# A Mamba block between two expert networks on one core: inverse roots on ScalarE, B and C projected in four column groups, a seventh C product on GpSimd, scans ahead of products on VectorE

## The reference

```python
x = x + 0.5 * ffn(layernorm(x))      # "f1"
x = x + mamba(layernorm(x))          # "p"
x = x + 0.5 * ffn(layernorm(x))      # "f2"

# ffn: argmax over 8 gates picks one expert of 128 -> gelu -> 128
# mamba(x):
xn = rmsnorm(x) * norm_w             # 128 channels
xs, z = split(xn @ in_proj.T)        # 256 + 256
xs = silu(causal_conv4(xs) + b)
dt_x, B, C = split(xs @ x_proj.T)    # 128, 16, 16
dt = softplus(dt_x @ dt_proj.T + b)
h  = exp(dt * A) * h + (dt * xs) * B # for each of 256 x 16 states, along the tokens
y  = sum_n(h * C) + D * xs
return (y * silu(z)) @ out_proj.T + x
```

## Time and profile before

| what | value |
|---|---|
| median of 3 runs | 1233.87 us (1229.54, 1233.87, 1234.02) |
| profiled execution, its time | 1229.34 us |
| its span, first to last instruction | 1227.5 us |
| mean granted TensorE clock | 0.936 of full speed |
| busy in the span | PE 1085.6, DVE 1033.3, POOL 1026.2, ACT 916.8 us |

### The profile page before, as it was taken

How to read it: one execution, slowest core, us unless ns; L and a number is a source line. 1 busy time by engine, 2 the same in 40 slices (tenths; PEclk the granted TensorE clock), 3 DMA queues, 4 the chain that set the end, 5 groups by cost and what they waited for, 6 DMA issues and landing times.

```text
span 1227.5 us, 16326 instructions
## 1 busy us (share of the span) xinstructions
PE 1085.6 (88%) x5188; PEld 553.7 (45%) x5188; DVE 1033.3 (84%) x1681; ACT 916.8 (75%) x1349; POOL 1026.2 (84%) x756
## 2 busy tenths in 40 slices
PE   6897859798989999998989999998989996977778
PEld 3352425253535444554545445454545443423245
DVE  2318998899999989999999999998999999999910
ACT  2457576788989888888879888888889796774631
POOL 1248998989899998999998999989899999999600
PEclk9897969799999999999999999999999997958789
DMA  4052324324142423333151433242250424342000
GB/s 102 1 177 85 137 104 140 112 82 161 29 156 104 146 103 140 104 125 136 51 177 61 146 106 146 95 156 104 73 184 24 166 86 146 99 153 95 1 9 18
DMA packets 60406, 130.03 MB, mean 106 GB/s; under 512 B 7744, under 2 KB 26864, under 8 KB 52128
## 3 DMA queue, kind: packets, MB, share of 16 engines
q1 hardware_dynamic: 60320, 128.98, 30.5%
HBM read 106.94 MB, written 22.02 MB: 105 GB/s over the span
## 4 chain that ended last, share of the span: by engine, by line
DVE 43%; PE 27%; ACT 12%; issue 11%; POOL 6%; DVEq 0%; DMA 0%; POOLq 0%; ACTq 0%
DVE dA L986 19%; DVE hb L984 8%; PE PY L619 7%; DVE hb L990 6%; PE PH L586 5%; PE G L567 4%; ACT hs L801 3%; DVE stat L965 3%; POOL hb L1158 2%; PE Y L631 2%; PE dA L599 2%; PE Y L664 2%; ACT xn L758 2%; ACT dA L825 2%; DVE xs L1003 2%
## 5 line engine op out<-in xcount | busy, mean ns | idle before, releaser
L1158 POOL TENSOR_TENSOR hb<-dtx_rep,bs 128x1024 f32<-128x1024 f32 x256 | 598.2, 2359 | 4.9 <-PE Y L631 4.4
L825 ACT ACTIVATE dA<-dt_rep,A 128x512 f32<-128x512 f32 x512 | 344.5, 688 | 105.4 <-DVE hb L990 83.6
L986 DVE TENSOR_TENSOR_SCAN dA<-dA,hb 128x512 f32<-128x512 f32 x320 | 390.2, 1219 | 8.1 <-DVE oh L1028 3.2
L619 PEld LDWEIGHTS PY<-W,hs 128*128 128x128 f32 x2048 | 259.2, 194 | 82.4 <-issue 73.0
L619 PE MATMUL PY<-W,hs 128*128 128x128 f32 x2048 | 293.7, 288 | 0.0
L1166 POOL TENSOR_TENSOR hb<-hb,cs 128x1024 f32<-128x1024 f32 x96 | 225.9, 2361 | 35.0 <-DVE hb L984 35.0
L990 DVE TENSOR_TENSOR hb<-dA,cs 128x512 f32<-128x512 f32 x320 | 221.4, 692 | 22.6 <-DVE dA L986 0.5
L984 DVE TENSOR_TENSOR_SCAN hb<-dA,hb 128x512 f32<-128x512 f32 x192 | 223.5, 1205 | 15.9 <-ACT dA L825 15.8
L586 PE MATMUL PH<-xnT,W 128*128 128x512 f32 x396 | 230.4, 665 | 0.0
L779 ACT COPY hs<-PH 128x512 f32<-128x512 f32 x198 | 114.7, 579 | 106.0 <-PE PH L586 86.9
L631 PE MATMUL Y<-hb,Sel 128*32 128x512 f32 x1024 | 151.8, 664 | 34.6 <-POOL hb L1166 33.7
(11 more groups left out here) (103 smaller groups left out, 1225.5 us busy)
## 6 DMA issues: line engine op xcount, KB each, us to landing
dtx_rep<-dtx_rows SPq DMA_DIRECT2D x32, 1024.0 KB, 6.3
dt_rep<-dt_rows SPq DMA_DIRECT2D x32, 1024.0 KB, 8.0
bs<-bc_rows SPq DMA_DIRECT2D x64, 256.0 KB, 3.7
cs<-bc_rows SPq DMA_DIRECT2D x64, 256.0 KB, 3.6
dtx_rows<-dtx SPq DMA_DIRECT2D x32, 256.0 KB, 2.4
dt_rows<-dt SPq DMA_DIRECT2D x32, 256.0 KB, 2.4
X<-in_x SPq DMA_DIRECT2D x16, 256.0 KB, 3.1
out<-X SPq DMA_DIRECT2D x16, 256.0 KB, 2.4
```

Of the source, the lines that this page charges most:

```text
L619: last = nc.tensor.matmul(PY[:, P * j:P * (j + 1)], hs[:, w, e, P * j:P * (j + 1)], W2[:, e, :], start=False, stop=e == E - 1 and j == J - 1)
L825: nc.scalar.activation(dA[u % NA][:, :], dt_rep[:, h, g, :], ACT.Exp, scale=A[:, h, g, q:q + 1]).then_inc(decay, 1)
L986: nc.vector.tensor_tensor_scan(a, a, x_in_hb, 0.0, ALU.mult, ALU.add).then_inc(scan, 1)
L1158: nc.gpsimd.tensor_tensor(hb[:, s % HR], dtx_rep[:, h, 2 * m:2 * m + 2, :], bs[:, q, None, :].broadcast_to([P, 2, CH]), ALU.mult).then_inc ...
```

## The change

Four things are changed.

1. `inverse_root`: in steady iterations ScalarE makes the root for f1 and f2 as `exp(-0.5*ln(var+eps))` on 4 columns, two instructions that wait on each other (`log_and_root`, at ACT slots 12.5 and 4.5), and GpSimd only negates the mean and multiplies. For p, GpSimd makes both roots in one `pow` of 8 columns, from var+eps and from a variance that is put together first. The f2 root's place on GpSimd is slot 6.5, before 5.5.
2. The products with the bias rows of W2 (L617) come all four ahead of the first expert's four products, before one by one between them. The projection onto B and C is made as eight matmuls of 32 x 128 in four column groups, before two of 32 x 512, and so the copy to SBUF is 128 x 128 instead of 32 x 512; the DMA that stores it writes the same bytes from 128 partitions.
3. Slot 4 joins POOL_C: its C product goes from VectorE to GpSimd, where it stands one slot later than the others do, in slot 6, ahead of slot 5's.
4. VectorE makes both scans of a slot and then both products, before scan, product, scan, product.

```diff
@@ STEADY
-    act={"silu": 3.0, "bc": 4.0, ..., "norm_f2": 7.5, "res_p": 13.5, ...
+    act={"silu": 3.0, "bc": 4.0, ..., "norm_f2": 7.5, "root_f2": 4.5, "root_f1": 12.5, "res_p": 13.5, ...
-    pool={"root_f2": 5.5, "dt": 7.0, "dtx": 7.5, "root_p": 11.0, "norm_p": 11.0, "root_f1": 12.5},
+    pool={"root_f2": 6.5, "dt": 7.0, "dtx": 7.5, "root_p": 11.0, "norm_p": 11.0, "root_f1": 12.5},
...
-POOL_C = (1, 2, 5, 9, 12, 14)
+POOL_C = (1, 2, 4, 5, 9, 12, 14)
+LATE_C = (4,)
...
+                for j in range(J if e == 0 else 0):
+                    nc.tensor.matmul(PY[:, P * j:P * (j + 1)], ohT[:, w, (it.i0 + off) % 2, P * j:P * (j + 1)],
+                                     b_part[:, 1, :], start=j == 0, stop=False)
                 for j in range(J):
-                    if e == 0:
-                        nc.tensor.matmul(PY[:, P * j:P * (j + 1)], ohT[:, w, (it.i0 + off) % 2, P * j:P * (j + 1)],
-                                         b_part[:, 1, :], start=j == 0, stop=False)
...
-                    product(it, "bc", 2 * N, [(Wbc[:, h, :], xsc[:, h, :]) for h in range(HF)])
+                    for h in range(HF):
+                        for g in range(GG):
+                            last = nc.tensor.matmul(G[b][2 * N * g:2 * N * (g + 1), 0:P], Wbc[:, h, :],
+                                                    xsc[:, h, P * g:P * (g + 1)], start=h == 0, stop=h == HF - 1)
...
+            def log_and_root(it, w, off):
+
+                k = 2 * act_roots(w, it.i0 + off)
+                it.wait(act, moments[w], off, 1, 1)
+                it.wait(act, normed[w], off, 1, 0)
+                nc.scalar.activation(vt[:, w, :], mv[:, w, :, 1], ACT.Ln, bias=eps[:, 0:1]).then_inc(log_root[w], 1)
+                act.wait_ge(log_root[w], k + 1)
+                nc.scalar.activation(rstd[:, w, :], vt[:, w, :], ACT.Exp, scale=-0.5).then_inc(log_root[w], 1)
...
-            def state_unit(it, u):
+            def state_scan(it, u):
...
+            def state_products(it, s):
+
                 if s in POOL_C:
                     return
+                q = place(s)[1]
+                it.wait(dve, c_in[q], 0, 16, 16)
+                for u in (2 * s, 2 * s + 1):
+                    it.wait(dve, scan, 0, UN, u + 1)
+                    nc.vector.tensor_tensor(hb[:, s % HR, u % 2, :], dA[u % NA][:, :], cs[:, q, :], ALU.mult) \
+                        .then_inc(prod, 1)
...
                     if it.has(0):
-                        state_unit(it, 2 * s)
+                        state_scan(it, 2 * s)
                     stages(it, s + 0.25)
                     if it.has(0):
-                        state_unit(it, 2 * s + 1)
+                        state_scan(it, 2 * s + 1)
+                        state_products(it, s)
...
+            def inverse_roots_p(it, off):
...
+                nc.gpsimd.tensor_tensor(roots[:, :, :], var[:, :, :], half[:, :, :], ALU.pow).then_inc(pool_ln[2], 1)
```

More of the change, by code:

```diff
@@ L208, in direct_no, with root_on_act, act_roots, roots_before @@
     return E * DIRECT.index((w, chunk)) + e
+def root_on_act(w, chunk):
+    return plan_of(chunk - ROOT_OFF[w]) is STEADY
+def act_roots(w, chunk):
+    return sum(root_on_act(w, c) for c in range(chunk))
+def roots_before(w, chunk):
+    return sum(1 if root_on_act(w, c) else 3 for c in range(chunk))
 def on_pool(s):
@@ L560, in transposes, with product @@
                 last.then_inc(g_full[b], 1)
-            def product(it, name, rows, terms):
+            def product(it, name, terms):
                 b = BANK[name]
@@ L566, in product @@
                 for k, (lhsT, rhs) in enumerate(terms):
-                    last = nc.tensor.matmul(G[b][0:rows, :], lhsT, rhs, start=k == 0, stop=k == len(terms) - 1)
+                    last = nc.tensor.matmul(G[b][:, :], lhsT, rhs, start=k == 0, stop=k == len(terms) - 1)
                 last.then_inc(g_full[b], 1)
@@ L742, in _, with copy_out @@
         def _(act):
[L743 removed]
+            def copy_out(it, name, dst, n=CH):
                 b = BANK[name]
                 it.wait_full(act, g_full, name)
[L747 removed]
+                nc.scalar.copy(dst, G[b][:, 0:n]).then_inc(g_free[b], 1)
             def rows(it, off, j):
@@ L837, in stages @@
                         copy_out(it, f"ln_f{w + 1}", xnT[:, w, :])
+                if t == at.get("root_f2") and it.has(-1):
+                    log_and_root(it, 1, -1)
+                if t == at.get("root_f1") and it.has(4):
+                    log_and_root(it, 0, 4)
                 if t == at.get("norm_f2") and it.has(-1):
@@ L1120, in inverse_root @@
                     .then_inc(pool_ln[w], 1)
-                nc.gpsimd.tensor_tensor(vt[:, w, :], mv[:, w, :, 1], eps[:, 0], ALU.add).then_inc(pool_ln[w], 1)
-                it.wait(pool, pool_ln[w], off, m, 2)
-                nc.gpsimd.tensor_tensor(rstd[:, w, :], vt[:, w, :], half[:, :], ALU.pow).then_inc(pool_ln[w], 1)
-                it.wait(pool, pool_ln[w], off, m, 3)
-                if w < 2:
-                    nc.gpsimd.tensor_tensor(shift[:, w, :], neg[:, w, :], rstd[:, w, :], ALU.mult).then_inc(rooted[w], 1)
-                    return
@@ L1199, in body @@
                         state_bx(it, 0, u)
-                    off, t = (0, s - 1) if s else (-1, SLOTS - 1)
-                    if it.has(off) and t in POOL_C:
-                        product_c(it, off, t)
+                    for back in (2, 1):
+                        off, t = (0, s - back) if s >= back else (-1, SLOTS + s - back)
+                        if it.has(off) and t in POOL_C and (t in LATE_C) == (back == 2):
+                            product_c(it, off, t)
                     stages(it, s + 0.5)
```

78 lines of the change are left out of this document (43 added, 35 removed).

## The result

The changed kernel takes 1241.14 us (median of 5 runs, 1240.23 to 1241.30) against 1233.87 for the kernel before in 5 runs (1229.1 to 1235.82). The ratio is 1.0069, with a 95% interval from 1.0043 to 1.0094: it is slower by 0.7%. The profiled execution took 1240.82 us, with a span of 1239.0 and a mean granted TensorE clock of 0.915.

What follows compares the result with a forecast made beforehand. VectorE, GpSimd and TensorE, each 94% busy, bound the kernel through their waits for each other. Ten iterations at -0.57 (-5.7) and -5 at fill and end: 1233.9 - 10.7 = 1223, put at 1222; 8 in 10: 1206 to 1240.

Steps and rivals of the forecast that it cites:

- third case: TensorE's longer wait after the taps: half clock in each iteration delays the next gelus by 2.4; 1243 us, chance 0.16.
- Sum: Whole kernel: -5.7 us over ten steady iterations and -5 in fill and end, so 1233.9 - 10.7 = 1223.
- this rival: TensorE's wait after the taps: the clock falls in every iteration, seven more falls at 1.4; 1233 us, chance 0.2.
- The rest of the sum: One steady iteration: slot 10 starts 1.2 earlier, then +0.1, +0.89 and -0.36, giving -0.57 us.
- Slots 10 to 14: dA banks come free 0.89 later: unit 24 is 0.1 later and the convolution starts 0.89 later.
- Slot 15, "0.36 less": Slot 15 ends 0.36 us earlier and starts the next gelus, by unit 31's product, last in either order.
- Slot 3: Products 6 and 7 stand behind the output projection's add: 0.5 us more from the add to slot 4.
- TensorE's gain, 1.2: Before slot 10: bias products save 0.8, B and C 0.7, less 0.3 for slot 4's late C product.
- VectorE would begin slot 10 earlier, but its add needs TensorE: VectorE could begin slot 10 1.95 us earlier, but TensorE is back to back from slot 1 to slot 11.
- GpSimd: Seventh product +2.3, roots -3.6, net -1.3 us an iteration; pow of 8 takes 2.0, waits up some 3.
- Fill and drain, -5: Outside the steady iterations: p root twice at -1.2, bias products about 1, VectorE freer at the end; together -5 us.
- ring free: ScalarE's slack hides the later dA banks, so VectorE's 4.8 counts: 2.5 us an iteration; 1204 us, chance 0.14.

Runs made afterwards that it cites:

- changed, filled: The changed kernel with three zero-weight float32 matmuls added in TensorE's wait ahead of slot 15's first expert product, iterations 2 to 12: 1222.12 us.
- the mixed one: The changed kernel with scan, product, scan, product in slots 0, 3, 10, 13 and both scans first in slots 6, 7, 8, 11, 15: 1211.48 us.
- the control: The mixed one with three zero-weight matmuls in iterations 2 to 12, placed in slot 7, where TensorE doesn't stand: 1239.08 us.

## Why the prediction was wrong

The prediction was 1222 us, faster; the outcome is that of its third case, "The same, and slower", 1243, which it gave 0.16. It lies 1.1 us above the range for 8 in 10, 1206 to 1240.

**The step that failed: the clock in "Sum".** The sum carried the falls of before over unchanged. The prediction had itself worked out that the stand would grow, by 0.8 because TensorE comes earlier and by 0.89 because ScalarE comes later, but then treated what follows as a rival. The stand grew by 1.0, and each iteration has a fall. Of its two terms the first came and the second hardly did: TensorE's edits made the stand 0.87 longer in the kernel before (1.91 to 2.78) and the new order 0.16 (1.91 to 2.07). In the changed kernel the stand ends 1.06 later behind slot 10's add, as ScalarE is that much later, but TensorE doesn't come earlier: behind that add it waits 0.36 for slot 9's C product and 0.83 instead of 0.37 for a copy, and so it reaches the stand 20.66 us behind the add, where it was 20.64, although the bias products save it 0.9 in between. The price of the falls comes from filling: 69.86 - 68.05 = 1.8 us an iteration for the changed kernel, 68.38 - 67.8 = 0.6 for before. Of the 1.48 us by which an iteration became longer, 1.2 is the clock. "HAM oscillation" on the page "TensorE: Matmul & The Clock Gate" of the Trainium skill, which the prediction set beside this rival, was the better guide: the traces of the changed kernel agree with it in direction, with ten falls in ten iterations and none once the stand is filled. They don't agree in all: the waits in the page's example are longer than the 2.95 us here, and in the kernel before a stand of 1.91 had a fall in four iterations of ten, not each time.

**The rest of the sum: -0.57 forecast, about +0.2 measured.** This is read from marks in a quiet iteration of either kernel. VectorE in the changed kernel with three zero products (add of f1, taps, add of the output projection, add of f1):

```profile
543.75 0.69 DVE L1089 SCALAR_TENSOR_TENSOR X<-PY,X 128x512 f32<-128x512 f32 x1 [1.23 <-PE PY L637]
...
566.21 2.72 DVE L1049 SCALAR_TENSOR_TENSOR xs<-G,Wc,xs 128x506 f32<-128x506 f32 x4 [1.70 <-ACT xs L893]
...
587.81 0.69 DVE L1089 SCALAR_TENSOR_TENSOR X<-Y,X 128x512 f32<-128x512 f32 x1 [0.94 <-PE Y L682]
...
611.76 0.69 DVE L1089 SCALAR_TENSOR_TENSOR X<-PY,X 128x512 f32<-128x512 f32 x1 [1.23 <-PE PY L637]
```

The same marks in the kernel before, from 684.00 on (the taps are at 705.39 in the earlier trace rows):

```profile
684.00 0.69 DVE L1043 SCALAR_TENSOR_TENSOR X<-PY,X 128x512 f32<-128x512 f32 x1
...
726.79 0.69 DVE L1043 SCALAR_TENSOR_TENSOR X<-Y,X 128x512 f32<-128x512 f32 x1
...
751.81 0.69 DVE L1043 SCALAR_TENSOR_TENSOR X<-PY,X 128x512 f32<-128x512 f32 x1
```

| stretch | before | changed, filled | difference | forecast |
|---|---|---|---|---|
| slot 10's add to the taps | 21.39 | 22.46 | +1.07 | +0.1 + 0.89 |
| taps to slot 3's add | 21.40 | 21.60 | +0.20 | -0.36 |
| slot 3's add to slot 10's add | 25.02 | 23.95 | -1.07 | -1.2 |

The changed kernel itself, unfilled, has the first and the third stretch at the same 22.46 and 23.95. All that its falls cost lies between the taps and slot 3's add: 22.81 us with a fall of 3.4 (713.22 to 736.03 above) and 24.26 with one of 6.8:

```profile
642.55 2.72 DVE L1042 SCALAR_TENSOR_TENSOR xs<-G,Wc,xs 128x506 f32<-128x506 f32 x4 [1.70 <-ACT xs L887]
...
666.81 0.69 DVE L1082 SCALAR_TENSOR_TENSOR X<-Y,X 128x512 f32<-128x512 f32 x1 [0.94 <-PE Y L681]
```

The kernel before takes 22.8 there too when its clock falls for 3.4 us. So the +0.20 of the middle row shows only while the clock stays up; with a fall TensorE sets this stretch in both kernels.

- *Slots 10 to 14.* Right. In slot 10 the products start 2.25 behind the scans and take 1.27, as forecast. The 0.42 before the taps became 1.70; slot 12's first scan waits 0.79.
- *Slot 15, "0.36 less".* Wrong, and the larger part of the miss. "By unit 31's product, which is last in either order" is true of the product, and leaves out ScalarE's queue. ScalarE in the filled kernel:

```profile
639.87 0.69 ACT L863 ACTIVATE dA<-dt_rep,A 128x512 f32<-128x512 f32 x1 [2.37 <-DVE hb L1035]
640.50 0.58 ACT L817 COPY hs<-PH 128x512 f32<-128x512 f32 x1
640.98 1.30 ACT L863 ACTIVATE dA<-dt_rep,A 128x512 f32<-128x512 f32 x2
```

  and in the kernel before:

```profile
710.14 0.69 ACT L825 ACTIVATE dA<-dt_rep,A 128x512 f32<-128x512 f32 x1 [1.47 <-DVE hb L990]
...
711.29 0.59 ACT L779 COPY hs<-PH 128x512 f32<-128x512 f32 x1 [0.46 <-PE PY L619]
711.94 1.30 ACT L825 ACTIVATE dA<-dt_rep,A 128x512 f32<-128x512 f32 x2
```

  The first decay of the next iteration waits for slot 15's *first* product, which the new order makes 0.9 later (5.64 from the taps instead of 4.75), and a copy of PH stands between it and the two decays ahead of the gelus. So these two decays start 6.75 from the taps instead of 6.55, and the gelus 0.2 later too: +0.2 where the sum has -0.36. The prediction applied its own rule ("all that stands behind that decay moves too") to slots 10 and 13 and not here.
- *Slot 3.* The wait for TensorE is 0.94 and VectorE's side costs about the 0.5 forecast; as forecast it is slack, since TensorE sets this stretch.
- *TensorE's gain, 1.2.* Measured 1.07, and that it came so near is luck, out of terms that were off. The bias products gain 0.95 (forecast 0.8). B and C take 0.62, 1.2 less than before (forecast 0.7 less), but right behind them TensorE waits 1.08 for ScalarE's copy of PH, which was not foreseen, so 0.1 of it is left. The 0.3 for slot 4's late product was nothing in this stretch; the one wait for GpSimd, 0.36, is for slot 9's and stands behind slot 10's add.
- *"VectorE would begin slot 10 earlier, but its add needs TensorE"* held: the wait there is 1.23.
- *GpSimd.* The pow of 8 columns took 1.65 (forecast 2.0), and its idle time rose from 4.1 to 6.8 an iteration (forecast "some 3" more). The roots on ScalarE take 0.29 + 0.21, the 0.5 forecast.

The changed kernel's page has these groups (busy us, mean ns, idle before):

```profile
L1180 POOL TENSOR_TENSOR roots<-var,half 128x8 f32<-128x8 f32 x16 | 26.5, 1653 | 1.3
...
L790 ACT ACTIVATE vt<-mv,eps 128x4 f32<-128x4 f32 x27 | 7.8, 289 | 0.0
...
L792 ACT ACTIVATE rstd<-vt 128x4 f32<-128x4 f32 x27 | 5.6, 206 | 0.9
```

- *Fill and drain, -5.* The span outside the ten iterations went from 543.7 to 540.4, so -3.3.

With the clock at +1.2 and the rest at +0.25 instead of -0.57, ten iterations give 14.8, less 3.3: the 11.5 by which the span grew. The "ring free" rival is out. The third case had the mechanism and the place (double-length products behind the stand, next gelus later) and put 2.4 on a fall; over the quiet iteration it measures 1.8 on average. That its 1243 came near 1241 is partly luck: it asked too much for a fall and kept the gain of 10.7 us from the rest, of which 0.8 are left in the profiled executions (3.3 outside the ten iterations, less 2.5 in them).

What stays open: why falls of 3.4 and 6.8 us take turns in the changed kernel, and why a stand of 1.9 is followed by a fall in some iterations and not in others.

## What to carry to other kernels

A saving on TensorE's list just ahead of a wait for another engine bought no time here; it made the stand longer, and the clock fell in more iterations behind it. Look first at what ends the stand, and if nothing can be done there, put work into it: three products with zeros in it were worth 19 us on the changed kernel (1241 to 1222) and 9 on the mixed one (1211 to 1203), and on the mixed one the same three elsewhere cost 28 (1211 to 1239).

In a ring of buffers an order that is shorter in total can still be the slower one, since the neighbour waits for the first buffer to come back and not for the sum. Scans first saved VectorE 0.36 us a slot and cost the kernel 2.2%; kept for the slots behind which nothing late hangs, the times show no clear gain (1214 to 1211, with intervals that overlap), and iterations with a fall of 3.4 us are some 0.3 us shorter (67.9 against 68.1 in most of them). Follow a later release down the neighbour's whole list, over the border of the iteration too.

## What the runs showed of the hardware

- Stands of 2.65 to 2.95 us were followed by a stretch at 1.2 GHz in eight to ten of ten iterations, one of 1.9 in three, four and six (three kernels), one of 2.1 in ten (the new order alone), and a filled one in none or one. The length of the stand alone doesn't decide it: the control had 2.5 and four falls, the mixed order 2.5 and eight.
- Zero products count as work for the clock: with three or four of them in the changed kernel's stand none of the ten iterations had a fall (window above, for three, at 1.00).
- A fall lasted 3.4 or 6.8 us. With TensorE's edits alone an iteration took 67.8 us without one, 69.2 with 3.4 and 70.7 with 6.8.
- A float32 product of 128 x 128 by 512 columns took 0.90 to 0.94 us, in two records (3.60 for four, 2.74 for three, 1.88 for two).
- B and C in four column groups, sixteen records of 128 columns, took 0.62 us where four of 512 columns took 1.88. "Key Properties" on the page "TensorEngine Tiling (Array Packing)" of the Trainium skill says that tiles work independently, and this agrees. What a change of mode costs can't be read here: the state sum ahead is in the same mode, and behind the product TensorE waits 1.08 us for ScalarE in any case.
- Alternating bf16 bias products with float32 pairs cost 2.3 us for one expert, the same work in two blocks 1.4 (634.10 to 635.51 in the timeline of the changed kernel).
